# Score units moved between the halves of key and value products in a perceiver cross-attention kernel

## The chip, the cores and the metric

The kernel runs on one core of one Trainium2 chip. The metric is device time in microseconds (us) of one launch; three runs of the kernel before gave 1930.27, 1930.81 and 1931.47 us. All stage times below are of one profiled execution of the same program.

## The reference, cut to what matters

```python
x = x + xattn(layernorm(x), ctx, ctx)       # x: 256 x 512, ctx: 25088 x 512, 16 heads of 32
x = x + attn(layernorm(x))                  # linear causal attention, 256 rows
x = x + ffn(layernorm(x))                   # ternary weights, hidden 2048

def xattn(query, key, value):
    q = (query @ Wq.T).reshape(1, 256, 16, 32) * 32 ** -0.5
    k = (key @ Wk.T).reshape(1, 25088, 16, 32)
    v = (value @ Wv.T).reshape(1, 25088, 16, 32)
    scores = sigmoid(einsum('blhd,bshd->bhls', q, k))      # no softmax, so chunks of s only add up
    return einsum('bhls,bshd->blhd', scores, v).reshape(1, 256, 512) @ Wo.T
```

Only the cross-attention is touched by the change. It takes most of the time, as the 25088 rows of context are walked in chunks.

## The kernel before, in words

The context is cut into 49 chunks of 512 rows. While chunk c is scored and weighed, the keys and values of chunk c+1 are made. TensorE does four kinds of work, and they take turns in the order in which they are written in the function for TensorE:

* **Key and value products.** Keys and values of a chunk come from seven half-size block products each (a Strassen-like scheme), called K1 to K7 and V1 to V7 here. A key product (k_product, matmul at L725) is 12 matmuls of 256 columns into the one PSUM tile kp, six for its upper row block (r = 0) and six for its lower (r = 1). A value product (v_product, L746) is the same into vp. The operands are split in a rounded part and a rest, hence three terms.
* **Score units** (scores, L761): four matmuls over 96 rows into one of two PSUM tiles sc0 and sc1, which take turns. A chunk has 16 units, numbered n = 0 to 15; pair(p) issues units 2p and 2p+1. Unit n waits until the sigmoid of unit n-2 has read its tile.
* **Weighing** (weigh, L781): eight matmul instructions per unit, which multiply the sigmoids of a unit (tile probs, a ring of nine) with the values and add to acc. The units are weighed in long stretches, as a change between this kind and the others costs something.

Two chunks make one pass of the loop, 22 passes in all (chunks 1 to 44); an "odd" chunk (par 1) comes first, then an "even" one (par 0). Chunks 45 and 46 follow with the same order but without the scan described below. Chunk 0 and chunk 47 use an order of their own, called alone here, and chunk 48 only scores and weighs; the change keeps all three as they were.

What the other engines do for it, each in its own fixed order, which the change does not touch:

* **ScalarE**, per chunk: sigmoids of units 0 and 1 (L376); k_part, a copy of K1 out of kp (L380), then v_part, a copy of V1 out of vp (L384); sigmoids 2 and 3; k_first and v_first, copies after K2 and V2 (L390, L394), then the issue of the load of a later chunk of context (L482); then sigmoids 4 to 15. In the even chunk of a pass two loads of a piece of weights are issued after sigmoid 6 and two after sigmoid 14 (L469).
* **VectorE**: k_first_rest after K2 (L570). After each product i from 3 to 7 first k_summed(i), which adds kp to an earlier part (L576) and from i = 5 on also rounds the sum (L589) and takes the rest (L591), then v_summed(i), which adds vp (L597). In the even chunk v_summed(3) is followed by the combinations 1 and 2 of the chunk after the next (a cast L526 and a subtraction L513 each), v_summed(4) by combination 3 with two sums ahead of it (L500, L502, L526, L513), and v_summed(5) and v_summed(7) by two scans each of the loaded pieces (L603). Combinations 4 to 7 (with the sums L505 and L508) come at the start of the next chunk, ahead of k_first_rest.
* **SyncE** moves the rounded keys by DMA into the stacked tile that the scores read.

TensorE's products wait for the tile they write to be read: K2 waits for k_part, V2 for v_part, K3 for k_first_rest, V3 for v_first, and K_i and V_i with i over 3 for k_summed(i-1) and v_summed(i-1). In the code these are

```python
elif i == 2:
    pe.wait_ge(kt_saved, m)                      # K2: k_part on ScalarE
elif i == 3:
    pe.wait_ge(k11_lo, m + 1)                    # K3: k_first_rest on VectorE
elif i > 3:
    pe.wait_ge(k_sum, (m - 1) * 5 + (i - 3))     # K4..K7: the sum of the product before
```

Of the kernel before, what the change touches and what calls it, by code (L numbers as in the profile page):

```python
# [105 lines left out]
def cross_attention(nc, x, ctxT, wqT, wkT, wvT, woT, wqk, wv, bv, wo, w_all, biases, keep):  # L106
# [5 lines left out]
    with ExitStack() as stack:  # L112
        def sb(name, shape, dt=F32):
            return stack.enter_context(nc.sbuf_tensor(name, shape, dt))

        def sem(name):
            return stack.enter_context(nc.semaphore(name))
# [8 lines left out]
        xc = sb("x_combos", [P, 7, 2, 2, HS], F32R)  # L126
        gap("before_more_weights", 16)
        more_w = sb("more_weights", [P, 7, 2, 2, HE], F32R)
        wk, wv_c = [first_w[:, i] for i in range(7)], [more_w[:, i] for i in range(7)]
# [53 lines left out]
        x_step, x_hi, x_ready = sem("x_step"), sem("x_hi"), sem("x_ready")  # L183
        k_made, kt_saved, k11_hi, k11_lo = sem("k_made"), sem("kt_saved"), sem("k11_hi"), sem("k11_lo")
# [5 lines left out]
        v_made, vt_saved, v11_saved, v_sum = sem("v_made"), sem("vt_saved"), sem("v11_saved"), sem("v_sum")  # L190
# [46 lines left out]
        N = TC * G  # L237
# [6 lines left out]
        def place(par, n):  # L244

            return PLACE[unit_of(par, n) % RING_U]
# [446 lines left out]
        def _(pe):  # L693
            pe.wait_ge(zeros_ready, 1)
            keep_clock(nc, keep, kp[:], 11)
            for b in range(G * L // 512):
                nc.tensor.matmul(acc[:, 2 * b:2 * b + 2, :], zeros[:, 0:P], zeros[:], start=True, stop=True,
                                 skip_group_check=True)
# [8 lines left out]
            TERMS = ((0, 0), (1, 0), (0, 1))  # L707
            FRESH = (1, 3, 6)

            def k_product(m, i, first=False):  # L710
                if i == 1 and first:
                    pe.wait_ge(k_lo, 3)
                elif i == 1:
                    pe.wait_ge(k_sum, (m - 1) * 5)
                elif i == 2:
                    pe.wait_ge(kt_saved, m)
                elif i == 3:
                    pe.wait_ge(k11_lo, m + 1)
                elif i > 3:
                    pe.wait_ge(k_sum, (m - 1) * 5 + (i - 3))  # L720
                n = 0
                for r in range(2):
                    for a, b in TERMS:
                        for k in range(2):
                            last = nc.tensor.matmul(k2[:, r, :], wk[i - 1][:, k, a, r * P:(r + 1) * P],  # L725
                                                    xc[:, i - 1, k, b, :], start=i in FRESH and n == 0, stop=n == 11,
                                                    skip_group_check=True)
                            n += 1
                last.then_inc(k_made, 1)

            def v_product(m, i, first=False):
                if i == 1 and first:
                    pe.wait_ge(v0_saved, 4)
                elif i == 1:
                    pe.wait_ge(v_sum, (m - 1) * 5)
                elif i == 2:
                    pe.wait_ge(vt_saved, m)
                elif i == 3:
                    pe.wait_ge(v11_saved, m)
                elif i > 3:  # L740
                    pe.wait_ge(v_sum, (m - 1) * 5 + (i - 3))
                n = 0
                for r in range(2):
                    for a, b in TERMS:
                        for k in range(2):
                            last = nc.tensor.matmul(v2[:, r, :], xc[:, i - 1, k, b, r * P:(r + 1) * P],  # L746
                                                    wv_c[i - 1][:, k, a, :], start=i in FRESH and n == 0, stop=n == 11,
                                                    skip_group_check=True)
                            n += 1
                last.then_inc(v_made, 1)  # L750

            def scores(c, n, order, free):
                t, g = order[n]
                if free:
                    pe.wait_ge(probs_ready, c * (TC * G) + (n - 1))
                if t % 2 == 0 and g % 2 == 0:
                    q = {(0, 0): 0, (0, 2): 1, (2, 2): 2, (2, 0): 3}[t, g]
                    pe.wait_ge(lo_moved[q], c * MOVED + MOVED)
                    pe.wait_ge(hi_twice[q], c * 16 + 16)
                for j in range(HG):  # L760
                    last = nc.tensor.matmul(sc[g % 2][:, j * L:(j + 1) * L],  # L761
                                            kst[0:3 * D, t // 2, g // 2, j, g % 2, t % 2 * P:(t % 2 + 1) * P],
                                            qst[0:3 * D, j, g, :], start=True, stop=True)
                last.then_inc(scores_ready, 1)

            def weigh(c, par, units, order, first=False):
                for n in units:
                    t, g = order[n]
                    if n not in (units[0], N // 2):
                        pass  # L770
                    elif first:
                        pe.wait_ge(v0_saved, 2 if t < 2 else 4)
                    elif t < 2:
                        pe.wait_ge(v11_saved, c)
                        pe.wait_ge(v_sum, (c - 1) * 5 + 3)
                    else:
                        pe.wait_ge(v_sum, (c - 1) * 5 + 5)
                    pe.wait_ge(probs_ready, c * N + (n + 1))
                    for j in range(HG):
                        h = g * HG + j  # L780
                        last = nc.tensor.matmul(acc[D * j:D * (j + 1), g, :], v[:, par, t, h * D:(h + 1) * D],  # L781
                                                probs[:, place(par, n), j * L:(j + 1) * L], start=False, stop=False,
                                                skip_group_check=True)
                    last.then_inc(probs_used, 1)
# [55 lines left out]
            for g in range(G):  # L840
                for k in range(KE):
                    last = nc.tensor.matmul(sc[0][:, g * L:(g + 1) * L], wq_raw[:, k, g * P:(g + 1) * P],
                                            xnT[:, k, :], start=k == 0, stop=k == KE - 1)
# [8 lines left out]
            def one(c, par, first, k_next, split_next, looped):  # L852
                m = c + 1

                order = BY_HALF if k_next else BY_TILE

                def unit(n):
                    scores(c, n, order, not (first and n < 2))

                def pair(p):  # L860
                    unit(2 * p)
                    unit(2 * p + 1)

                def keys(i):
                    pe.wait_ge(x_ready, c * 7 + i)
                    k_product(m, i, first)

                if not k_next:
                    pair(0)
                    for p in range(2 * TC):  # L870
                        if p + 1 < 2 * TC:
                            pair(p + 1)
                        weigh(c, par, (2 * p, 2 * p + 1), order)
                    return
                alone = first or not split_next
                pair(0)
                keys(1)
                v_product(m, 1, first)
                pair(1)
                keys(2)  # L880
                v_product(m, 2)
                pair(2)
                if not alone and par == 0:
                    weigh(c - 1, 1, range(11, N), order)
                    weigh(c, 0, range(6), order)
                keys(3)
                v_product(m, 3)
                pair(3)
                keys(4)
                v_product(m, 4)  # L890
                if alone:
                    weigh(c, par, range(8), order, first)
                pair(4)
                keys(5)
                v_product(m, 5)
                if not alone and par == 1:
                    unit(10)
                    weigh(c, 1, range(11), order)
                    unit(11)
                else:  # L900
                    pair(5)
                keys(6)
                v_product(m, 6)
                pair(6)
                keys(7)
                pair(7)
                v_product(m, 7)
                if alone:
                    weigh(c, par, range(8, N), order, first)
                elif par == 0:  # L910
                    weigh(c, 0, range(6, N), order)

            chunks(pe, one)
            pe.wait_ge(wo_loaded, 16)

# [16 lines left out]
            for a, to in enumerate((kp, vp)):  # L932
                for g in range(G):
                    if a == 1 and g == G - 1:
                        transpose_norm(0)
                    pe.wait_ge(o_saved, g + 1)
                    last = nc.tensor.matmul(to[:], oT[:, g, a * P:(a + 1) * P], wo_sb[:, g, :],
                                            start=g == 0, stop=g == G - 1)
# [597 lines left out]
```

## Time and profile before

| | |
|---|---|
| runs | 1930.27, 1930.81, 1931.47 us |
| profiled execution | 1930.52 us, its span 1928.8 us, mean granted clock 0.999 |
| one pass (two chunks) | 68.2 to 68.4 us, 22 passes |
| PE busy / PEld busy | 99% / 89% of the span |
| DVE busy / ACT busy | 63% / 53% of the span |

PE is TensorE's matmuls, PEld its weight loads (one ahead of each matmul), DVE is VectorE, ACT is ScalarE. The ends of matmuls are modelled, so the starts of the weight loads are the better clock for TensorE: the time from the first load of one stretch to the first load of the next is what the stretch costs. In the stretches of products and scores these loads follow one another every 0.113 to 0.118 us.

### The profile page before, as it was taken

Reading aid. Unit: us, or ns where it says so; the run is one execution under the profiler, and the core shown is the slowest. Engines: PE = TensorE matmul, PEld = TensorE weight load, DVE = VectorE, ACT = ScalarE, POOL = GpSimd, SP = SyncE. Lnnn points to the kernel's source line nnn. Section 1 sums busy time; section 2 is a strip of 40 time slices with the busy share of each in tenths; the row PEclk is TensorE's granted clock in tenths of the full one; section 3 lists DMA queues with packets and bytes.
Section 4 is the critical chain, followed back from the end, with each engine's and each line's share of the span. In section 5 each row is a group of like instructions: output and inputs, shape, how many; then the busy total and the mean of one; then the engine's idle time right before and its main releaser. Section 6 shows DMA issues by size and latency. Waiting matters only on the chain. (4 is left out here: it accounts for less than half of the span.)

```text
span 1928.8 us, 50817 instructions
## 1 busy us (share of the span) xinstructions
PE 1913.4 (99%) x19362; PEld 1716.6 (89%) x19362; DVE 1212.3 (63%) x2113; ACT 1014.3 (53%) x1132; POOL 4.3 (0%) x16
## 2 busy tenths in 40 slices
PE   8999999999999999999999999999999999999999
PEld 7989999998899999989899999988999999857998
DVE  7566776767667676766767667676676766336322
ACT  5545555555545555454455555555455554544764
POOL 0000000000000000000000000000000000000000
PEclk9999999999999999999999999999999999999999
DMA  7556555665655656565565656656556564554774
GB/s 212 148 157 169 137 153 156 158 158 145 170 142 150 166 140 165 139 164 147 156 166 138 155 154 158 156 151 166 145 146 165 145 163 104 110 211 168 278 278 161
DMA packets 128395, 310.92 MB, mean 161 GB/s; under 512 B 33888, under 2 KB 33888, under 8 KB 109664
## 3 DMA queue, kind: packets, MB, share of 16 engines
q1 hardware_dynamic: 95952, 214.10, 43.8%
q10 hardware_dynamic: 32400, 96.22, 15.1%
q8 instruction: 30, 0.49, 0.1%
q14 instruction: 13, 0.11, 0.0%
HBM read 153.95 MB, written 0.52 MB: 80 GB/s over the span
## 5 line engine op out<-in xcount | busy, mean ns | idle before, releaser
L376 ACT ACTIVATE probs<-sc 128x1024 f32<-128x1024 f32 x784 | 769.4, 1025 | 719.6 <-PE sc L761 578.3
L725 PE MATMUL kp<-x_combos,weights_r 128*128 128x256 f32 x4032 | 519.7, 278 | 0.0
L746 PE MATMUL vp<-more_weights,x_combos 128*128 128x256 f32 x4032 | 518.5, 277 | 0.0
L725 PEld LDWEIGHTS kp<-x_combos,weights_r 128*128 128x128 f32 x4032 | 486.9, 188 | 9.5 <-issue 9.5
L746 PEld LDWEIGHTS vp<-more_weights,x_combos 128*128 128x128 f32 x4032 | 488.2, 188 | 0.0
L761 PE MATMUL sc<-rows_r,k_stack_r 96*128 96x256 f32 x3136 | 438.3, 281 | 0.8 <-ACT probs L376 0.8
L761 PEld LDWEIGHTS sc<-rows_r,k_stack_r 96*128 96x128 f32 x3136 | 394.2, 188 | 24.6 <-issue 21.8
L576 DVE TENSOR_TENSOR parts<-parts,kp 128x512 f32<-128x512 f32 x240 | 164.6, 686 | 321.3 <-PE kp L725 321.3
L781 PE MATMUL acc<-probs,v 128*32 128x256 f32 x6272 | 355.2, 380 | 0.0
L781 PEld LDWEIGHTS acc<-probs,v 128*32 128x32 f32 x6272 | 195.5, 110 | 131.7 <-ACT probs L376 0.4
L513 DVE TENSOR_TENSOR x_combos<-ctx_raw,x_combos 128x512 fp32r<-128x512 f32 x240 | 166.2, 692 | 8.2
L603 DVE TENSOR_TENSOR bits<-bits,weights 128x512 int32<-128x512 int32 x176 | 121.3, 689 | 45.2 <-DMA weights<-w_all_dram 41.4
L597 DVE TENSOR_TENSOR v<-parts,vp 128x512 f32<-128x512 f32 x144 | 98.7, 686 | 55.7 <-PE vp L746 55.7
L526 DVE CAST x_combos<-ctx_raw 128x512 fp32r<-128x512 f32 x240 | 101.3, 422 | 4.5 <-DMA ctx_raw<-ctxT_dram 0.8
L591 DVE TENSOR_TENSOR k_rows_lo<-parts,k_rows_hi 128x512 fp32r<-128x512 f32 x144 | 99.7, 692 | 5.0
L1306 ACT ACTIVATE w_hi<-w_raw 128x2048 fp32r<-128x2048 f32 x42 | 80.0, 1907 | 0.0
L589 DVE CAST k_rows_hi<-parts 128x512 fp32r<-128x512 f32 x144 | 61.6, 428 | 23.4 <-DMA k_stack_r<-k_rows_lo 12.3
L597 DVE TENSOR_TENSOR v<-v,vp 128x512 f32<-128x512 f32 x96 | 65.7, 684 | 10.1 <-PE vp L746 8.4
L513 DVE TENSOR_TENSOR x_combos<-x_sum,x_combos 128x512 fp32r<-128x512 f32 x96 | 66.5, 693 | 3.3
L570 DVE TENSOR_TENSOR k_rows_lo<-kp,k_rows_hi 128x512 fp32r<-128x512 f32 x48 | 33.2, 692 | 52.9 <-ACT k_rows_hi L390 52.9
L1422 PE MATMUL ps<-weights_r,w_hi 128*128 128x256 f32 x512 | 60.5, 279 | 0.0
L1422 PEld LDWEIGHTS ps<-weights_r,w_hi 128*128 128x128 f32 x512 | 60.4, 188 | 0.0
(159 smaller groups left out, 858.6 us busy)
## 6 DMA issues: line engine op xcount, KB each, us to landing
k_stack_r<-k_rows_hi SPq DMA_DIRECT2D x784, 64.0 KB, 2.4
k_stack_r<-k_rows_lo SPq DMA_DIRECT2D x784, 64.0 KB, 2.5
k_stack_r<-k_stack_r SPq DMA_DIRECT2D x196, 256.0 KB, 3.0
ctx_raw<-ctxT_dram ACTq DMA_DIRECT2D x47, 1024.0 KB, 6.4
weights<-w_all_dram ACTq DMA_DIRECT2D x176, 256.0 KB, 3.3
w_raw<-w_all_dram SPq DMA_DIRECT2D x44, 1024.0 KB, 4.8
weights<-wqk_dram SPq DMA_DIRECT2D x2, 1024.0 KB, 9.9
probs<-wkT_dram SPq DMA_DIRECT2D x2, 512.0 KB, 5.3
```

The lines of the kernel that those rows point to most:

```text
L376: nc.scalar.activation(probs[:, place(par, n), :], sc[g % 2][:], ACT.Sigmoid).then_inc(probs_ready, 1)
L513: nc.vector.tensor_tensor(xc[:, i - 1, :, 1, :], x_source(raw, i), f32(xc[:, i - 1, :, 0, :]), ALU.subtract).then_inc(x_ready, 1)
L526: nc.vector.tensor_copy(xc[:, i - 1, :, 0, :], x_source(raw, i)).then_inc(x_hi, 1)
L576: nc.vector.tensor_tensor(to, kc[:, K_PART[add], :, :], k2, ALU.add).then_inc(k_sum, 1)
L591: nc.vector.tensor_tensor(kr_lo[:, at, :, :], to, f32(kr_hi[:, at, :, :]), ALU.subtract).then_inc(k_lo, 1)
L597: nc.vector.tensor_tensor(v_at(par, q), vt[:] if add == "t" else v_at(par, add), v2, ALU.add).then_inc(v_sum, 1)
L603: nc.vector.tensor_tensor(bits[:], bits[:], piece[:, t % 2, :], ALU.bitwise_or).then_inc(piece_used, 1)
L725: last = nc.tensor.matmul(k2[:, r, :], wk[i - 1][:, k, a, r * P:(r + 1) * P], xc[:, i - 1, k, b, :], start=i in FRESH and n == 0, stop=n = ...
L746: last = nc.tensor.matmul(v2[:, r, :], xc[:, i - 1, k, b, r * P:(r + 1) * P], wv_c[i - 1][:, k, a, :], start=i in FRESH and n == 0, stop=n ...
L761: last = nc.tensor.matmul(sc[g % 2][:, j * L:(j + 1) * L], kst[0:3 * D, t // 2, g // 2, j, g % 2, t % 2 * P:(t % 2 + 1) * P], qst[0:3 * D, ...
L781: last = nc.tensor.matmul(acc[D * j:D * (j + 1), g, :], v[:, par, t, h * D:(h + 1) * D], probs[:, place(par, n), j * L:(j + 1) * L], start ...
L1422: last = nc.tensor.matmul(ps[q][:, 0, :], wt[:, k, :], x[:, k, :], start=m == 0, stop=m == passes * KH - 1)
```

## The change

TensorE's order in the odd and in the even chunk is written out anew; the alone order and the last chunk are kept. The waits themselves, every other engine's program, all tiles and the number of matmuls are kept. A product can now be issued in two calls, row block 0 (six matmuls, with the wait ahead) and row block 1 (six matmuls, with the increment behind). Let a and b be the two halves, p0 to p7 the pairs, u10 and u11 single units, W a stretch of weighing with its number of units:

```text
odd before : p0 K1 V1 p1 K2 V2 p2 K3 V3 p3 K4 V4 p4 K5 V5 u10 W11 u11 K6 V6 p6 K7 p7 V7
odd after  : K1a p0 K1b V1 p1 K2 V2 p2 K3 V3 p3 K4 V4 p4 K5 V5 u10 W11 K6a u11 K6b V6 p6 K7 V7a p7 V7b
even before: p0 K1 V1 p1 K2 V2 p2 W11 K3 V3 p3 K4 V4 p4 K5 V5 p5 K6 V6 p6 K7 p7 V7 W10
even after : K1 p0 V1 K2a p1 K2b V2 p2 W11 K3a p3 K3b V3 K4a p4 K4b V4 K5 p5 V5 K6 V6a p6 V6b K7 V7 p7 W10
```

The core of the diff:

```diff
-            def k_product(m, i, first=False):
-                if i == 1 and first:
+            def k_product(m, i, first=False, rows=(0, 1)):
+                if rows[0] == 1:
+                    pass
+                elif i == 1 and first:
...
-                n = 0
-                for r in range(2):
+                for r in rows:
+                    n = 0
                     for a, b in TERMS:
                         for k in range(2):
                             last = nc.tensor.matmul(k2[:, r, :], wk[i - 1][:, k, a, r * P:(r + 1) * P],
-                                                    xc[:, i - 1, k, b, :], start=i in FRESH and n == 0, stop=n == 11,
-                                                    skip_group_check=True)
+                                                    xc[:, i - 1, k, b, :], start=i in FRESH and r == 0 and n == 0,
+                                                    stop=r == 1 and n == 5, skip_group_check=True)
                             n += 1
-                last.then_inc(k_made, 1)
+                if rows[-1] == 1:
+                    last.then_inc(k_made, 1)
...
+                def keys_around(i, scored, n):
+                    keys(i, (0,))
+                    scored(n)
+                    keys(i, (1,))
+                def values_around(i, scored, n):
+                    values(i, (0,))
+                    scored(n)
+                    values(i, (1,))
...
+                def odd():
+                    keys_around(1, pair, 0)
+                    values(1)
+                    pair(1)
...
+                    unit(10)
+                    weigh(c, 1, range(11), order)
+                    keys_around(6, unit, 11)
+                    values(6)
+                    pair(6)
+                    keys(7)
+                    values_around(7, pair, 7)
+
+                def even():
+                    keys(1)
+                    pair(0)
+                    values(1)
+                    keys_around(2, pair, 1)
+                    values(2)
+                    pair(2)
                     weigh(c - 1, 1, range(11, N), order)
                     weigh(c, 0, range(6), order)
+                    keys_around(3, pair, 3)
+                    values(3)
+                    keys_around(4, pair, 4)
+                    values(4)
+                    keys(5)
+                    pair(5)
+                    values(5)
+                    keys(6)
+                    values_around(6, pair, 6)
+                    keys(7)
+                    values(7)
+                    pair(7)
+                    weigh(c, 0, range(6, N), order)
```

## Rows read from the trace of the kernel before

**Rows 1.** The page: busy time, share of the span and instructions of each engine.

```profile
PE 1913.4 (99%) x19362; PEld 1716.6 (89%) x19362; DVE 1212.3 (63%) x2113; ACT 1014.3 (53%) x1132; POOL 4.3 (0%) x16
```

**Rows 2.** One pass: its length, busy PE, PEld, DVE, ACT, POOL, then granted clock, DMA.

```profile
894.85:963.22 68.37, 68.37 (x724) 61.76 (x720) 46.47 (x79) 35.68 (x40) 0.00 (x0) 1.00 0.59 153
```

**Rows 3.** Timeline of PEld, odd chunk after W11: start, us, what, xcount.

```profile
918.79 0.53 PEld L761 LDWEIGHTS sc<-rows_r,k_stack_r 96*128 96x128 f32 x4 [0.41 <-issue]
919.25 1.49 PEld L725 LDWEIGHTS kp<-x_combos,weights_r 128*128 128x128 f32 x12
...
922.08 1.00 PEld L761 LDWEIGHTS sc<-rows_r,k_stack_r 96*128 96x128 f32 x8
923.00 1.44 PEld L725 LDWEIGHTS kp<-x_combos,weights_r 128*128 128x128 f32 x12
924.37 1.02 PEld L761 LDWEIGHTS sc<-rows_r,k_stack_r 96*128 96x128 f32 x8
925.32 1.49 PEld L746 LDWEIGHTS vp<-more_weights,x_combos 128*128 128x128 f32 x12
```

**Rows 4.** Timeline, start of the even chunk: ACT, then PEld.

```profile
927.62 1.94 ACT L376 ACTIVATE probs<-sc 128x1024 f32<-128x1024 f32 x2 [0.52 <-PE sc L761]
929.44 0.60 ACT L380 ACTIVATE parts<-kp 128x512 f32<-128x512 f32 x1
...
933.09 0.60 ACT L390 ACTIVATE k_rows_hi<-kp 128x512 fp32r<-128x512 f32 x1
...
926.74 1.01 PEld L761 LDWEIGHTS sc<-rows_r,k_stack_r 96*128 96x128 f32 x8
927.68 1.44 PEld L725 LDWEIGHTS kp<-x_combos,weights_r 128*128 128x128 f32 x12
929.04 1.44 PEld L746 LDWEIGHTS vp<-more_weights,x_combos 128*128 128x128 f32 x12
...
931.33 1.44 PEld L725 LDWEIGHTS kp<-x_combos,weights_r 128*128 128x128 f32 x12
```

**Rows 5.** Timeline: two waits whose release the trace shows, on PE and on DVE.

```profile
35.04 0.69 DVE L563 TENSOR_TENSOR k_rows_lo<-kp,k_rows_hi 128x512 fp32r<-128x512 f32 x1 [2.98 <-ACT k_rows_hi L420]
...
35.84 0.54 PEld L808 LDWEIGHTS kp<-x_combos,weights_r 128*128 128x128 f32 x4 [0.68 <-issue]
...
933.94 0.69 DVE L570 TENSOR_TENSOR k_rows_lo<-kp,k_rows_hi 128x512 fp32r<-128x512 f32 x1 [0.49 <-ACT k_rows_hi L390]
```

**Rows 6.** Timeline of PEld, even chunk from K3 to W10.

```profile
940.07 1.48 PEld L725 LDWEIGHTS kp<-x_combos,weights_r 128*128 128x128 f32 x12 [0.41 <-issue]
...
946.55 1.00 PEld L761 LDWEIGHTS sc<-rows_r,k_stack_r 96*128 96x128 f32 x8
...
956.20 1.02 PEld L761 LDWEIGHTS sc<-rows_r,k_stack_r 96*128 96x128 f32 x8
957.15 1.49 PEld L746 LDWEIGHTS vp<-more_weights,x_combos 128*128 128x128 f32 x12
958.77 0.16 PEld L781 LDWEIGHTS acc<-probs,v 128*32 128x32 f32 x8
```

**Rows 7.** Timeline of DVE, even chunk: the sums of V4, V5 and V6.

```profile
946.86 0.69 DVE L597 TENSOR_TENSOR v<-parts,vp 128x512 f32<-128x512 f32 x1 [0.24 <-PE vp L746]
...
951.76 0.68 DVE L597 TENSOR_TENSOR v<-parts,vp 128x512 f32<-128x512 f32 x1
...
955.64 0.68 DVE L597 TENSOR_TENSOR v<-v,vp 128x512 f32<-128x512 f32 x1
```

**Rows 8.** Timeline of DVE: second scan behind W10's start; the pass before, odd chunk.

```profile
962.34 0.69 DVE L603 TENSOR_TENSOR bits<-bits,weights 128x512 int32<-128x512 int32 x1 [0.60 <-DMA weights<-w_all_dram]
...
894.10 0.69 DVE L603 TENSOR_TENSOR bits<-bits,weights 128x512 int32<-128x512 int32 x1 [0.70 <-DMA weights<-w_all_dram]
...
899.98 0.69 DVE L513 TENSOR_TENSOR x_combos<-ctx_raw,x_combos 128x512 fp32r<-128x512 f32 x1
902.04 0.69 DVE L570 TENSOR_TENSOR k_rows_lo<-kp,k_rows_hi 128x512 fp32r<-128x512 f32 x1 [1.36 <-ACT k_rows_hi L390]
```

More of the change, by code:

```diff
@@ L725, in k_product, with v_product @@
                             last = nc.tensor.matmul(k2[:, r, :], wk[i - 1][:, k, a, r * P:(r + 1) * P],
-                                                    xc[:, i - 1, k, b, :], start=i in FRESH and n == 0, stop=n == 11,
-                                                    skip_group_check=True)
+                                                    xc[:, i - 1, k, b, :], start=i in FRESH and r == 0 and n == 0,
+                                                    stop=r == 1 and n == 5, skip_group_check=True)
                             n += 1
-                last.then_inc(k_made, 1)
-            def v_product(m, i, first=False):
-                if i == 1 and first:
+                if rows[-1] == 1:
+                    last.then_inc(k_made, 1)
+            def v_product(m, i, first=False, rows=(0, 1)):
+                if rows[0] == 1:
+                    pass
+                elif i == 1 and first:
                     pe.wait_ge(v0_saved, 4)
@@ L741, in v_product @@
                     pe.wait_ge(v_sum, (m - 1) * 5 + (i - 3))
-                n = 0
-                for r in range(2):
+                for r in rows:
+                    n = 0
                     for a, b in TERMS:
@@ L746, in v_product @@
                             last = nc.tensor.matmul(v2[:, r, :], xc[:, i - 1, k, b, r * P:(r + 1) * P],
-                                                    wv_c[i - 1][:, k, a, :], start=i in FRESH and n == 0, stop=n == 11,
-                                                    skip_group_check=True)
+                                                    wv_c[i - 1][:, k, a, :], start=i in FRESH and r == 0 and n == 0,
+                                                    stop=r == 1 and n == 5, skip_group_check=True)
                             n += 1
-                last.then_inc(v_made, 1)
+                if rows[-1] == 1:
+                    last.then_inc(v_made, 1)
             def scores(c, n, order, free):
@@ L862, in pair, with keys, values, weighing @@
                     unit(2 * p + 1)
[L864 to L868, printed above, removed]
+                def keys(i, rows=(0, 1)):
+                    if rows[0] == 0:
+                        pe.wait_ge(x_ready, c * 7 + i)
+                    k_product(m, i, first, rows)
+                def values(i, rows=(0, 1)):
+                    v_product(m, i, first, rows)
+                def keys_around(i, scored, n):
[6 more added lines that the diff above has]
+                    values(i, (1,))
+                def weighing():
                     pair(0)
@@ L873, in one, with alone @@
                         weigh(c, par, (2 * p, 2 * p + 1), order)
[L874 to L883, printed above, removed]
+                def alone():
+                    pair(0)
+                    keys(1)
+                    values(1)
+                    pair(1)
+                    keys(2)
+                    values(2)
+                    pair(2)
+                    keys(3)
+                    values(3)
+                    pair(3)
+                    keys(4)
+                    values(4)
+                    weigh(c, par, range(8), order, first)
+                    pair(4)
+                    keys(5)
[7 more added lines that the diff above has]
+                    values(7)
+                    weigh(c, par, range(8, N), order, first)
@@ new lines, in odd @@
+                def odd():
+                    keys_around(1, pair, 0)
+                    values(1)
+                    pair(1)
+                    keys(2)
+                    values(2)
+                    pair(2)
+                    keys(3)
+                    values(3)
+                    pair(3)
+                    keys(4)
+                    values(4)
+                    pair(4)
+                    keys(5)
+                    values(5)
+                    unit(10)
+                    weigh(c, 1, range(11), order)
+                    keys_around(6, unit, 11)
+                    values(6)
+                    pair(6)
+                    keys(7)
+                    values_around(7, pair, 7)
@@ L884, in one @@
+                def even():
+                    keys(1)
+                    pair(0)
+                    values(1)
+                    keys_around(2, pair, 1)
+                    values(2)
+                    pair(2)
                     weigh(c - 1, 1, range(11, N), order)
                     weigh(c, 0, range(6), order)
[L886 to L899, printed above, removed]
-                else:
[L901 to L911, printed above, removed]
+                    keys_around(3, pair, 3)
@@ new lines, in even @@
+                    values(3)
+                    keys_around(4, pair, 4)
+                    values(4)
+                    keys(5)
+                    pair(5)
+                    values(5)
+                    keys(6)
+                    values_around(6, pair, 6)
+                    keys(7)
+                    values(7)
+                    pair(7)
+                    weigh(c, 0, range(6, N), order)
+                if not k_next:
+                    weighing()
+                elif first or not split_next:
+                    alone()
+                elif par == 1:
+                    odd()
+                else:
+                    even()
```

## The prediction

> **What bounds the kernel now.** I read the page's busy times first, then one pass of the loop by stretch, then the timelines of the weight loads, of ScalarE and of VectorE within that pass. The page shows TensorE at 99% and the others at 63% and 53%, [rows 1]. One pass shows the same: PE busy 68.37 of 68.37 us, at a granted clock of 1.00, the upper level of 2.4 GHz [rows 2]. So the time is TensorE's own issue, pass after pass, and the question is how much of a pass is not plain issue. The starts of the weight loads tell it. A product costs 1.36 to 1.37 us where TensorE runs freely (927.68 to 929.04 in rows 4, 923.00 to 924.37 in rows 3), but the two just behind a stretch of weighing cost 2.83 (919.25 to 922.08), so 1.41 or 1.42 each [rows 3]: 0.05 more. A pair of scores costs 0.92 (922.08 to 923.00), but 0.95 at p7 (924.37 to 925.32), which waits a little for its sigmoids, and V7 behind it again 1.42, up to p0 at 926.74 [rows 3, 4]. Each way out of weighing costs 0.41 idle [rows 3, 6], and the new order keeps as many of them. That is all there is to win. ScalarE and VectorE are no bound by their sums, but each is a queue in fixed order, and TensorE's products wait on points in it. The margin of those waits is the real question, as none of them is late now.
>
> **What the change may win.** In the odd chunk: K1a behind weighing at the slower pace (about 0.02 lost at the head); K6a, u11, K6b, V6, p6, K7, V7a, p7, V7b without the late pair: before 926.74 - 918.79 = 7.95 [rows 3, 4], after 0.71 + 0.46 + 0.71 + 1.41 + 0.92 + 1.37 + 0.68 + 0.92 + 0.68 = 7.86, so 0.09 won. In the even chunk: from K3 to W10 before 958.77 - 940.07 = 18.70 [rows 6]; without any wait five products of each kind (13.65 at 1.365), five pairs (4.6), the 0.2 that the turn to weighing costs and some 0.07 of slower pace would give 18.52, so 0.18 won. Together 0.25 a pass. A half product is priced at half of a whole, 0.68, and at the slow pace 0.71; no row shows a split product, so the bounds for its extra cost are nothing and one more 0.05 per product (the pace of rows 3); I take nothing, as the number of switches between products and scores hardly changes.
>
> **First cost: K2 of the even chunk.** K2 must wait for k_part, which ScalarE runs only behind the sigmoids of units 0 and 1. Before, p0, K1, V1 and p1 lay between the start of p0 and K2: K2 at 931.33, k_part done at 929.44 + 0.60 = 930.04 [rows 4]. That is 3.30 after the start of p0 at 926.74, against 4.59 for K2. In the new order K1 is ahead of p0, and only p0 and V1 lie between: 0.94 + 1.36 = 2.30 after the start of p0, K2a is at its wait. The 3.30 can't shrink with K1 earlier, since 0.88 passes until the first sigmoid can start (927.62), 1.82 for the two, and 0.60 for the copy [rows 4]. On top comes the release of the wait. The nearest row is a wait of TensorE for VectorE: that one ended at 35.04 + 0.69 = 35.73, and the load came at 35.84, 0.11 later; the bounds are 0 and the 0.25 between ScalarE's end at 933.69 and VectorE's start at 933.94 [rows 4, 5]. I take 0.11, as it is the same waiting engine. So TensorE stands still for 3.41 - 2.30 = 1.11, and K2a then runs at the slow pace (0.03): 1.14 a pass, bounds 1.0 and 1.3. Queued behind K2a on TensorE are p1, K2b, V2, p2 and W11, all moved by the full amount, and nothing on another engine can give it back, because W11 and all after it are issued in order.
>
> **Second cost: V6 and V7 of the even chunk.** VectorE is busy nearly without a break from V4's sum on. V4's stretch ended at 946.55 and its sum began 0.31 later (946.86); V6's sum ended at 955.64 + 0.68 = 956.32 [rows 6, 7]. In between are combination 3, K5's and K6's sums with their splits, V5's sum and two scans, 9.46 us. With the release V7 may start 0.31 + 9.46 + 0.11 = 9.88 after V4's stretch ends. Before, TensorE took 957.15 - 946.55 = 10.60 for what lies between [rows 6], a margin of 0.72. After, p4 lies ahead of V4's end and p7 behind V7: K5, p5, V5, K6, V6a, p6, V6b, K7 take 1.37 + 0.92 + 1.36 + 1.37 + 0.68 + 0.92 + 0.68 + 1.37 = 8.67. So 1.21 of waiting, spread over the same queue: K5 and K6 wait for the sums of K4 and K5, V6a for V5's sum (done 951.76 + 0.68 - 946.86 = 5.58 after V4's began, so at 6.00 where TensorE comes at 5.02), V7 for V6's. They don't add up; the last one sets the time. From the start of K3a: V4 ends at 7.33 (K3a at slow pace 0.71, p3, K3b, V3, K4a, p4, K4b, V4), V7 starts at 7.33 + 9.88 = 17.21, takes 1.42, p7 and the turn to weighing 1.13: W10 at 19.76 against 18.70 before, 1.06 more a pass, bounds 0.9 and 1.3. This figure already holds the 0.18 that could have been won there.
>
> The Trainium skill says (Perfetto Trace Analysis, Summary: the profiler window per engine type) that the profiler's window of an engine's instruction leaves out the time in which its semaphore spreads. The 0.11 above agrees with it; by the ends of the rows alone the first stall would be 1.00. The same page (Optimizing Tensor Performance, Matmuls) advises that matmul groups take turns over PSUM banks so that the reading of one overlaps the next. Keys and values do take turns here, and by that rule alone, a read of 0.69 behind a neighbour's 1.37, the second cost would be nothing; the rows show VectorE's queue, not the tile, as what is late.
>
> **Sum.** A pass: +0.02 - 0.09 + 1.14 + 1.06 = +2.13; 22 passes give 46.9. Chunks 45 and 46 have no scans: the first cost stays 1.14, V6a still waits 0.98 of which some 0.1 is won elsewhere, so about 2.0. In all 48.9. The profiled execution took 1930.5 (span 1928.8), 0.3 below the median: forecast 1930.5 + 48.9 = 1979.4, and 1979.7 beside the median. I say 1979.5.
>
> **Rivals.** (A) Only the first cost is real: VectorE's queue catches up. For it: the queue has 0.72 of margin now. Against: p4, p5 (by its place) and p7, which made that margin, are taken from exactly this stretch. A pass would be 1.14 - 0.07 - 0.18 = +0.89, 23 times 20.5: 1951. (B) The late p7 knocks on. The loads of the scanned pieces are issued behind sigmoid 14. The second scan began 962.34 - 956.20 = 6.14 after p7 did, so 0.88 ahead of the next p0 at 963.22 [rows 2, 6, 8]; p7 then starts 1.13 ahead of W10 instead of 2.57, so the scan is 1.44 later. Combinations 4 to 7 end 6.57 after the second scan begins (894.10 to 899.98 + 0.69), so 7.13 after the pass starts; k_first_rest needs 0.69 and 0.11 more: K3 may start at 7.93, and TensorE comes at 8.25 (three pairs, four products, 0.03 of slow pace). Now k_first_rest is done at 902.73, 7.88 after the pass's start at 894.85 [rows 2, 8]: about the same margin of 0.3, behind ScalarE. If the loads land 1 us later than in this pass, K3 waits 0.7 each time: 16 more, 1996. (C) Faster: the even spacing of the pairs brings its 0.25 a pass and no wait binds: 23 x 0.25 = 6 less, 1925. It needs k_part to be done within 2.30 of p0's start and VectorE's queue within 8.67 of V4's end; for it speaks only that the late p7 and the slow pace do cost something now. It decides from a release 1.1 earlier on ScalarE, which no row allows. (D) The product halves switch dearer than priced, 0.05 for each of the seven halved products of a pass with everything else as forecast: 8 more, 1987.5.
>
> **How the numbers follow.** Forecast 0.70, A 0.12, B 0.08, C 0.03, D 0.05, and 0.02 that costs and gains cancel. The forecast's own range is 1968 to 1988, from the bounds on the releases (0 to 0.25 twice a pass) and on VectorE's queue. The range that holds 8 in 10 takes in A: 1950 to 1988. About 0.2% is what a measurement of this kernel can tell from no change. Faster by over 0.2%: C, 0.03; within: 0.02; slower: 0.95.
>
> **What would show it.** In the profile after: a row of L725 in the even chunk with some 1 us idle ahead of it, put down to ScalarE's L380, once a pass, 23 in all; idle ahead of L746 and L725 put down to VectorE's L597 and L576, about 1.2 a pass together; passes of 70.4 us in place of 68.3; V3 behind K3b at the fast 1.36; p7 of both chunks at 0.92 without a wait. The page's PE busy share would fall by about two points. If K2a follows V1 at 0.11, the first step is wrong and the whole forecast falls; if V6a and V7 follow at once, A is right; if K3 of the odd chunk shows a wait for L570, B is.

## The result, and the profile after

The changed kernel takes 1978.07 us (median of four runs, 1977.57 to 1978.87) against 1931.06 before: ratio 1.0248, 95% interval 1.0236 to 1.0260. The forecast was 1979.5, within 1950 to 1988. A few runs of most kernels are 4 to 6 us lower than the rest (1925.33 beside a median of 1931.20 for the kernel before) and stay in the medians, and one of the kernel before, 3016.06 us at a granted clock of 0.592, is left out of the ratios.

First the page of the profile after: span, busy times, clock. PE does the same matmuls and loses a point of its share, but its busy time grows by 25.8 us: the rows of matmuls stretch over part of the waiting, so the starts of the weight loads are again the better clock. The granted clock is 1.000 in the mean, its upper level.

```profile
span 1976.4 us, 50816 instructions
PE 1939.2 (98%) x19361; PEld 1727.4 (87%) x19362; DVE 1209.8 (61%) x2113; ACT 1012.6 (51%) x1132; POOL 4.3 (0%) x16
PEclk9999999999999999999999999999999999999999
```

One pass of the loop by stretch (its length, then busy PE, PEld, DVE, ACT, POOL, the clock, DMA). It answers to [rows 2]: 70.31 us where a typical pass took 68.24, and PE is no longer busy throughout. (The 68.37 of [rows 2] is one of three passes of the kernel before that are 0.13 longer than its others.)

```profile
919.60:989.91 70.31, 69.33 (x725) 62.10 (x721) 46.19 (x78) 35.58 (x40) 0.00 (x0) 1.00 0.59 149
```

Twenty-two passes at 2.07 more are 45.5 us, and the last odd and even chunk without scans bring the rest of 47.0: W10 of chunk 46 began at 1688.4 in place of 1641.1. From the start of the last W10 to the end the two kernels take nearly the same, 288.0 and 287.7.

**The first place: K2a of the even chunk.** The timeline of the weight loads (start, duration as merged, what, count), then that of ScalarE over the same stretch. It answers to [rows 4].

```profile
951.25 1.48 PEld L728 LDWEIGHTS kp<-x_combos,weights_r 128*128 128x128 f32 x12
952.66 1.00 PEld L769 LDWEIGHTS sc<-rows_r,k_stack_r 96*128 96x128 f32 x8
953.59 1.48 PEld L753 LDWEIGHTS vp<-more_weights,x_combos 128*128 128x128 f32 x12
956.07 0.76 PEld L728 LDWEIGHTS kp<-x_combos,weights_r 128*128 128x128 f32 x6 [1.00 <-DVE x_combos L513]
...
960.85 4.47 PEld L789 LDWEIGHTS acc<-probs,v 128*32 128x32 f32 x88
...
953.53 1.94 ACT L376 ACTIVATE probs<-sc 128x1024 f32<-128x1024 f32 x2 [1.19 <-PE sc L769]
955.35 0.60 ACT L380 ACTIVATE parts<-kp 128x512 f32<-128x512 f32 x1
```

V1 takes from 953.59 to 956.07, 2.48 in place of 1.36: a hole of 1.12 ahead of K2a. The copy of K1 (L380) ends at 955.95 by its row, and the load comes 0.12 later; unrounded, and over 22 passes, it is 0.11 each time. The row of the load itself names VectorE's L513, which is a trap: two waits stand ahead of K2a, one for combination 2 of the context (L513) and one for the copy of K1. Combination 2 was ready at 941.41; the instruction of L513 that ended shortly before K2a belongs to a later combination. The list of waits of TensorE (engine, line, waited for: us in total, times, longest) has both:

```profile
PE kp L728 <- ACT parts L380: 18.9, 23, 0.8
```

```profile
PEld kp L728 <- DVE x_combos L513: 22.9, 23, 1.0
PEld vp L753 <- DVE v L597: 7.1, 23, 0.3
PEld kp L728 <- DVE parts L576: 5.6, 22, 0.3
```

Both counts are 23, once in each even chunk; that the copy is the true releaser was settled by moving it (below).

**The second place: K3 to W10 of the even chunk.** It answers to [rows 6, 7]: weight loads, then VectorE.

```profile
965.74 0.78 PEld L728 LDWEIGHTS kp<-x_combos,weights_r 128*128 128x128 f32 x6 [0.41 <-issue]
...
971.73 1.44 PEld L753 LDWEIGHTS vp<-more_weights,x_combos 128*128 128x128 f32 x12
973.19 1.48 PEld L728 LDWEIGHTS kp<-x_combos,weights_r 128*128 128x128 f32 x12
...
975.52 1.48 PEld L753 LDWEIGHTS vp<-more_weights,x_combos 128*128 128x128 f32 x12
977.26 1.48 PEld L728 LDWEIGHTS kp<-x_combos,weights_r 128*128 128x128 f32 x12 [0.26 <-DVE parts L576]
979.05 0.77 PEld L753 LDWEIGHTS vp<-more_weights,x_combos 128*128 128x128 f32 x6 [0.31 <-DVE v L597]
...
982.92 1.47 PEld L753 LDWEIGHTS vp<-more_weights,x_combos 128*128 128x128 f32 x12
...
985.45 1.66 PEld L789 LDWEIGHTS acc<-probs,v 128*32 128x32 f32 x34
```

```profile
973.40 0.69 DVE L597 TENSOR_TENSOR v<-parts,vp 128x512 f32<-128x512 f32 x1 [0.27 <-PE vp L753]
...
976.53 0.68 DVE L576 TENSOR_TENSOR parts<-parts,kp 128x512 f32<-128x512 f32 x1
...
978.31 0.68 DVE L597 TENSOR_TENSOR v<-parts,vp 128x512 f32<-128x512 f32 x1
...
982.18 0.68 DVE L597 TENSOR_TENSOR v<-v,vp 128x512 f32<-128x512 f32 x1
```

The stretch takes 985.45 - 965.74 = 19.71, against 18.70 before. K6 comes at 977.26, 0.05 after K5's sum (977.21); V6a at 979.05, 0.06 after V5's (978.99); V7 at 982.92, 0.06 after V6's (982.86). Ahead of K5, K6, V6a and V7 the weight loads are late by 0.10, 0.33, 0.38 and 0.12, 0.93 in all. From V3's sum to V6's, VectorE waits for TensorE only once, the 0.27 ahead of V4's sum. The stretch is 1.01 longer, though the waits come to 0.93: the rest is a slower pace of some products, to which I come below.

### The profile page after: what moved, and what is told of

Its sections match the earlier page's. It is cut to its first block and busy times, and to the rows that moved or that the text cites. A ratio compares the mean times of both kernels' runs of the same rounds, so it can differ in the third digit from the quotient of the medians.

```text
span 1976.4 us, 50816 instructions
## 1 busy us (share of the span) xinstructions
PE 1939.2 (98%) x19361; PEld 1727.4 (87%) x19362; DVE 1209.8 (61%) x2113; ACT 1012.6 (51%) x1132; POOL 4.3 (0%) x16
## 5 line engine op out<-in xcount | busy, mean ns | idle before, releaser
L728 PE MATMUL kp<-x_combos,weights_r 128*128 128x256 f32 x4032 | 554.0, 282 | 20.1 <-ACT parts L380 18.9
L728 PEld LDWEIGHTS kp<-x_combos,weights_r 128*128 128x128 f32 x4032 | 498.8, 188 | 57.7 <-issue 28.6
L753 PE MATMUL vp<-more_weights,x_combos 128*128 128x256 f32 x4032 | 530.1, 279 | 2.4
L769 PE MATMUL sc<-rows_r,k_stack_r 96*128 96x256 f32 x3136 | 432.1, 279 | 0.8 <-ACT probs L376 0.8
L513 DVE TENSOR_TENSOR x_combos<-ctx_raw,x_combos 128x512 fp32r<-128x512 f32 x240 | 166.2, 693 | 8.2
L513 DVE TENSOR_TENSOR x_combos<-x_sum,x_combos 128x512 fp32r<-128x512 f32 x96 | 66.4, 692 | 3.3
```

The source lines that it names most:

```text
L513: nc.vector.tensor_tensor(xc[:, i - 1, :, 1, :], x_source(raw, i), f32(xc[:, i - 1, :, 0, :]), ALU.subtract).then_inc(x_ready, 1)
L769: last = nc.tensor.matmul(sc[g % 2][:, j * L:(j + 1) * L], kst[0:3 * D, t // 2, g // 2, j, g % 2, t % 2 * P:(t % 2 + 1) * P], qst[0:3 * D, ...
```

## The experiments

Each kernel's time is a median; the kernel before, run beside each on the same chip, had medians of 1930.3 to 1931.4. All are the changed kernel with the edit shown unless it is said otherwise, and all keep the computation whole. The edits are shortened: calls that stand on lines of their own in the code share one here, and "..." marks a cut.

**K2 whole again, with p1 ahead of it.**

```diff
 def even():
-    keys(1); pair(0); values(1); keys_around(2, pair, 1); values(2); pair(2)
+    keys_around(1, pair, 0); values(1); pair(1); keys(2); values(2); pair(2)
```

> The changed kernel with the head of the even chunk written as K1a p0 K1b V1 p1 K2 V2 p2 in place of K1 p0 V1 K2a p1 K2b V2 p2: K2 gets p1 back ahead of it, all else as changed. Theory 1 (K2 waits for ScalarE's copy of K1, 1.12 us in each of 23 even chunks): K2 comes 3.88 us after p0 starts, the copy is released at 3.41, so the wait goes; p0 is now 2.3 behind p7 and may wait some 0.1 for sigmoid 15. 1978.1 - 23 x 1.05 = 1954. Theory 2 (VectorE's queue alone costs the time, and the wait at K2a only shifts it): the stretch from K3 to W10 would grow by what is won, 1978.

Measured 1951.2, a pass 69.15 in place of 70.31. The hole is gone, the stretch from K3 to W10 is unchanged at 19.7, so theory 2 is out and theory 1 holds. The time came out 3 lower than expected: p0 didn't wait (0.93), and V1 is at the fast pace again (1.36).

**The copy of K1 first, TensorE's order untouched.**

```diff
+early = par == 0 and split_next and not first
+if n == 0 and early:
+    k_part(m)
 sigmoid(c, par, n, at, first)
 if k_next and n == 1:
-    k_part(m)
+    if not early:
+        k_part(m)
```

> The changed kernel with TensorE's order untouched, and ScalarE's copy of K1 (k_part) put ahead of sigmoid 0 in the even chunks. Theory 1 (what is late at K2a is the copy's place in ScalarE's queue, behind two sigmoids): the copy is done 0.9 us after p0 starts, K2a follows V1 at once, 1978.1 - 23 x 1.14 = 1952. Theory 2 (what costs is K2 cut in two around a pair of scores, by itself): the gap at K2a stays and the time is 1978.

Measured 1954.0, a pass 69.26. ScalarE's and TensorE's rows at the place that had the hole:

```profile
940.32 0.60 ACT L380 ACTIVATE parts<-kp 128x512 f32<-128x512 f32 x1 [0.64 <-PE kp L732]
940.88 1.94 ACT L376 ACTIVATE probs<-sc 128x1024 f32<-128x1024 f32 x2
...
940.93 1.48 PEld L757 LDWEIGHTS vp<-more_weights,x_combos 128*128 128x128 f32 x12
942.35 0.78 PEld L732 LDWEIGHTS kp<-x_combos,weights_r 128*128 128x128 f32 x6
```

V1 to K2a is 1.42: no hole, though K2 is still cut around p1, VectorE's combinations are where they were, and only ScalarE's order changed. So the copy's place behind two sigmoids was the cause, neither the cut nor L513. The 0.05 to 0.06 over 1.36 is the slow pace; of the hole of 1.12 it leaves 1.07 of standing still.

**The second part of the even chunk as before.** K3 V3 p3 K4 V4 p4 K5 V5 p5 K6 V6 p6 K7 p7 V7 in place of the new order from K3 on.

> The changed kernel with the even chunk's second part, K3 to p7, in the order of the kernel before (K3 V3 p3 K4 V4 p4 K5 V5 p5 K6 V6 p6 K7 p7 V7); heads and odd chunk as changed. Theory 1 (two independent costs, 1.12 at K2a and 1.00 between K3 and W10): that stretch goes from 19.70 back to 18.70 us, 1978.1 - 23 x 1.0 = 1955, and K2a still waits 1.12. Theory 2 (one cost that the other follows from): near 1931 or no change, 1978.

Measured 1955.05: the stretch from K3 to W10 takes 18.66, and V1 to K2a still 2.48. The two costs are independent and add: 1978.1 - 1951.2 = 26.9 for the head and 23.0 for this part. Their sum, 49.9, is 2.9 more than the 47.0 of the change, as both runs keep the odd chunk's new order, which wins something: 31.65 us from its start to that of the even chunk in place of 31.76, 0.11 a pass or 2.5 in all.

**p4 behind V4.**

```diff
-    keys_around(4, pair, 4); values(4)
+    keys(4); values(4); pair(4)
```

> The changed kernel with one pair moved: K4 V4 p4 in the even chunk in place of K4a p4 K4b V4. Theory 1 (VectorE needs 9.88 us from the end of V4's stretch to V7, whatever stands between): V4 ends at 6.41 after K3a in place of 7.43, V7 may start at 16.29 in place of 17.2, TensorE's own work is 9.59 long there, so 0.3 of waiting is left of 1.2: W10 at 18.83 in place of 19.70, 1978.1 - 23 x 0.87 = 1958. Theory 2 (the waits belong to the split products or to the pairs' distance from their sigmoids): one pair's place changes little, 1974 to 1978.

Measured 1970.1: 8 us less, where theory 1 expected 20 and theory 2 at most 4. The weight loads behind V3, V4 and K7, then VectorE's timeline, say why.

```profile
965.24 1.48 PEld L728 LDWEIGHTS kp<-x_combos,weights_r 128*128 128x128 f32 x12
...
968.06 1.01 PEld L769 LDWEIGHTS sc<-rows_r,k_stack_r 96*128 96x128 f32 x8
...
978.39 1.48 PEld L753 LDWEIGHTS vp<-more_weights,x_combos 128*128 128x128 f32 x12
...
965.55 0.69 DVE L597 TENSOR_TENSOR v<-parts,vp 128x512 f32<-128x512 f32 x1 [0.68 <-PE vp L753]
...
968.28 0.68 DVE L576 TENSOR_TENSOR parts<-parts,kp 128x512 f32<-128x512 f32 x1
968.88 0.68 DVE L597 TENSOR_TENSOR v<-parts,vp 128x512 f32<-128x512 f32 x1
...
977.66 0.68 DVE L597 TENSOR_TENSOR v<-v,vp 128x512 f32<-128x512 f32 x1
```

V4 ended at 968.06, but its sum could not start until 968.88: VectorE was on V3's sum, combinations 1 and 2 and K4's sum without a break from 965.55 on. So V7 is bound twice. Here it comes 13.15 after V3's end (965.24 to 978.39) and 10.33 after V4's. In the changed kernel VectorE has the break of 0.27 ahead of V4's sum, so there V4's end binds, 9.83 ahead of V7 (973.09 to 982.92), and the bound from V3's end lies 0.36 earlier (969.41 + 13.15 = 982.56). With p4 moved back the bound from V3 takes over after 0.36; what is left of the cost belongs to p3 ahead of V3. The prediction had priced the bound that holds in the changed kernel, not the one close behind it.

**p3 behind V3, p4 between the halves of K4.**

```diff
-    keys_around(3, pair, 3); values(3)
+    keys(3); values(3); pair(3)
```

> The changed kernel with one pair moved: K3 V3 p3 in the even chunk in place of K3a p3 K3b V3; p4 stays between the halves of K4. What the run with p4 moved showed (1970 where 1958 was expected): VectorE's queue is busy from V3's sum on, so V7 is bound twice, by 13.2 us from the end of V3's stretch and by 9.88 from the end of V4's. Theory 1 (two bounds): V3's end comes 0.9 earlier but V4's stays, so nothing is won, 1977 to 1978. Theory 2 (p3 ahead of V3 is what costs, p4 doesn't matter): 13 us less, 1965.

Measured 2008.0, far outside both. The edit left only half a product between p3 and p4, and the waits of the weight loads show a new kind, which I had not looked for. The list of waits, then one even chunk from K4a to V7:

```profile
PEld sc L769 <- ACT probs L376: 26.6, 51, 0.9
```

```profile
985.26 0.76 PEld L728 LDWEIGHTS kp<-x_combos,weights_r 128*128 128x128 f32 x6
986.36 0.53 PEld L769 LDWEIGHTS sc<-rows_r,k_stack_r 96*128 96x128 f32 x4 [0.34 <-ACT probs L376]
987.61 0.53 PEld L769 LDWEIGHTS sc<-rows_r,k_stack_r 96*128 96x128 f32 x4 [0.72 <-ACT probs L376]
988.08 0.78 PEld L728 LDWEIGHTS kp<-x_combos,weights_r 128*128 128x128 f32 x6
...
990.19 1.48 PEld L728 LDWEIGHTS kp<-x_combos,weights_r 128*128 128x128 f32 x12
...
1000.01 1.47 PEld L753 LDWEIGHTS vp<-more_weights,x_combos 128*128 128x128 f32 x12
```

p4 begins 0.4 late and takes 1.71 in place of 0.92, as its units wait for the sigmoids of p3: 1.2 of the 1.3 that a pass is longer (71.61 for 70.31). The time can't decide between the two theories. The trace does bear on the first: counted from K3, V4 ends 1.33 later than in the changed kernel, and V7 comes 9.82 behind it (990.19 to 1000.01), the 9.83 of the changed kernel, though VectorE now stood idle for 1.64 between V3's sum and K4's. So the bound from V4's end holds by itself.

**Both pairs behind their value products.** K3 V3 p3 K4 V4 p4, from K5 on as changed.

> The changed kernel with both pairs moved: K3 V3 p3 K4 V4 p4 in the even chunk, and from K5 on as changed. Theory 1 (two bounds, from V3 and from V4): both are back where they were, some 0.2 of waiting is left in the stretch from K3 to W10, 18.8 in place of 19.70 us, 1978.1 - 23 x 0.9 = 1957, though either pair alone gives 8 or nothing. Theory 2 (the two moves add up, 8 for p4 and nothing for p3): 1970.

Measured 1958.75, the stretch from K3 to W10 18.84 us. So p3 and p4 ahead of V3 and V4 together make 0.86 of the second cost, and p4 alone, moved back, 0.34 (8 us). Theory 1 was off by 1.8, theory 2 by 11. The 0.14 over the 18.70 of before is not the waiting that was expected: no wait of TensorE for VectorE is left in the list, and it is the slow pace.

**Combination 3 late, TensorE's order untouched.**

```diff
-combos = ... {3: (1, 2), 4: (3,)}
+combos = ... {3: (1, 2), 7: (3,)}
```

> The changed kernel with TensorE's order untouched; on VectorE combination 3 of the even chunk (four instructions, 2.5 us) is moved from behind V4's sum to behind V7's, ahead of the two scans whose loads it waits for there. Theory 1 (V6 and V7 wait for VectorE's queue, which has dead time only behind V7's sum): V5's and V6's sums come 2.5 us earlier, of 0.93 waiting some 0.1 to 0.15 stays at K5 (combinations 1 and 2), and the scans still end when their loads land: 1978.1 - 23 x 0.8 = 1960. Theory 2 (the waits belong to the split products): no change, 1978; and if the dead time is needed, the next chunk's K3 waits, up to 1990.

Measured 1960.45, a pass 69.53. The waits at K6, V6a and V7 are gone, and the one at K5 (0.10) stays as expected. VectorE at the end of the even chunk:

```profile
975.30 0.68 DVE L597 TENSOR_TENSOR v<-v,vp 128x512 f32<-128x512 f32 x1
975.90 0.68 DVE L500 TENSOR_TENSOR ctx_raw<-ctx_raw 128x512 f32<-128x512 f32 x1
...
979.13 0.69 DVE L603 TENSOR_TENSOR bits<-bits,weights 128x512 int32<-128x512 int32 x1 [0.63 <-DMA weights<-w_all_dram]
```

The four instructions now fill the time in which VectorE stood waiting for the pieces; in the changed kernel that wait was 2.73 long at the first scan. The second cost is thus VectorE's queue, not the halves. But the prediction's rival B shows itself here: in four of 22 passes the loaded pieces land so late that the second scan begins 1.04 to 1.34 into the next pass (at most 0.80 in the changed kernel), and K3 of that odd chunk waits for k_first_rest, by up to 0.34:

```profile
849.32 1.48 PEld L728 LDWEIGHTS kp<-x_combos,weights_r 128*128 128x128 f32 x12 [0.27 <-DVE k_rows_lo L570]
```

**Both cures, and combination 1 early.** First the copy first and combination 3 late together; then also combination 1 of the even chunk behind the two scans at its start.

> The changed kernel with TensorE's order untouched, ScalarE's copy of K1 ahead of sigmoid 0 and VectorE's combination 3 behind V7's sum, both in the even chunks. Theory (the order itself is worth some 0.2 us a pass, and only the two queues took it back): no wait is left but 0.1 to 0.15 at K5, a pass takes 68.2 us as before or a little less, 1926 to 1931 against 1930.3 of the kernel before. Rival (the cures cost what they free elsewhere): 1935 to 1945.

> As the kernel with both cures, and combination 1 of the even chunk is moved from behind V3's sum to behind the scans at its start, in VectorE's idle stretch during W11. Theory: the wait at K5 goes too, a pass takes some 68.0 us, 1924 to 1927. Rival: the load of the context lands too late there and K4 waits for K3's sum, 1930 or more.

Measured 1936.15 (ratio to before 1.0029, interval 1.0018 to 1.0040) and 1934.87 (1.0022, 1.0012 to 1.0031). Both theories missed, and both times lie where the rivals had put them, though mostly not for the rivals' reasons. In the typical pass every wait but K5's 0.10 is gone in the first, K5's too in the second, and still a pass takes 68.46 and 68.37 where the kernel before has 68.24. In the second the odd chunk takes 0.11 less than before, but K1 to W11 takes 8.56 for 8.44 and K3 to W10 18.81 for 18.71, all of it slow pace. So the new order by itself costs 0.13 a pass; it does not win 0.25. What the rivals feared comes in single passes and adds under 1 us to the profiled executions: K3 of the odd chunk is late in two of 22 passes of the first run (by up to 0.24) and one of the second, and in two of the second K4 waits 0.4 for K3's sum, behind a combination 1 that waits for its load of the context.

The profiled execution of the second run took 1930.34, less than its median. Its passes are the 68.37 above; what is short is the time from the start of the last W10 to the end, 283.8 us in place of 288.1 in the first. The cause was not looked for.

**Where the expected gain went.** In all these traces the products run at two paces, 0.1135 and 0.1178 us a matmul (1.36 and 1.41 a product), and where no wait stands the slow one begins at the same places: where a value product or half of one follows scores (V6b, V7b, V7 of the kernel before), and where a key product follows a value product with no scores between (V7b K1, V3 K4a, V4 K5, V6b K7). It ends where a key product follows scores or goes on behind them. It also begins behind W11 (K3a and K6a take 0.70). To test it away from waits, one pair was moved in the kernel before, in the odd chunk, where there is room:

```diff
-    values(3); pair(3); keys(4)
+    values_around(3, pair, 3); keys(4)
```

> The kernel before with one pair moved in the odd chunk: V3a p3 V3b K4 in place of V3 p3 K4. No wait binds there by a wide margin for K4 (2.3 us after K3 ends, its sum needs 1.1). Theory 1 (the slow pace of 0.118 us a matmul starts where a value product follows scores or a key product follows a value product with no scores between, and ends where a key product follows scores): V3b takes 0.706, K4 and V4 1.41 each, fast again from K5 on; 0.12 a pass, 1931 + 2.7 = 1934. Theory 2 (the slow pace is left over from a wait or a late semaphore): V3b 0.68, K4 1.36 as before, at most V4 slow, 1931 to 1932.

Measured 1934.26 (1.0016, interval 1.0004 to 1.0029). The weight loads from V3a to V5:

```profile
906.19 0.76 PEld L753 LDWEIGHTS vp<-more_weights,x_combos 128*128 128x128 f32 x6
906.87 1.00 PEld L769 LDWEIGHTS sc<-rows_r,k_stack_r 96*128 96x128 f32 x8
907.79 0.78 PEld L753 LDWEIGHTS vp<-more_weights,x_combos 128*128 128x128 f32 x6
908.50 1.48 PEld L728 LDWEIGHTS kp<-x_combos,weights_r 128*128 128x128 f32 x12
909.91 1.49 PEld L753 LDWEIGHTS vp<-more_weights,x_combos 128*128 128x128 f32 x12
911.33 1.00 PEld L769 LDWEIGHTS sc<-rows_r,k_stack_r 96*128 96x128 f32 x8
912.25 1.44 PEld L728 LDWEIGHTS kp<-x_combos,weights_r 128*128 128x128 f32 x12
```

V3a 0.68, V3b 0.71, K4 1.41, V4 1.42, and K5 behind p4 1.37 again, in all 22 passes: as theory 1 said, at this place. Why a matmul is 0.004 dearer there is not shown, and the pattern is not a full rule. K6 behind the single unit u11, straight after weighing, is slow in the kernel before (1.415), while K1a behind W10 is fast in the changed one (0.68). K1 and V1 of the odd chunk, behind p0, are slow in 3 of 22 passes of the kernel before and in 9 of 22 of this run, with the same order in every pass. And a wait can start the slow pace too: K3 behind a late p2 takes 1.40 to 1.41 in four passes of the run with combination 3 late. So theory 2 is out for V3b and K4, not as a second cause elsewhere.

**The kernel before with what was found.** From the changed order only K6a u11 K6b in the odd chunk, and combination 3 late, which takes away the small wait of V6; else the kernel before.

> The kernel before with two things taken over: K6a u11 K6b in place of u11 K6 in the odd chunk, and VectorE's combination 3 behind V7's sum in the even chunk. From the changed kernel's table, K6 and V6 behind W11 cost 3.22 us in place of 3.29, and without the small wait V6 of the even chunk (1.40) goes to 1.36: 0.10 to 0.12 a pass, 1931 - 2.6 = 1928. Rival (the halves and the place of the combination bring nothing of their own): 1930 to 1931.

Measured 1927.39 in eleven runs against 1931.38, ratio 0.9973, interval 0.9962 to 0.9984: small, but faster than both kernels. A pass takes 68.12 in place of 68.24: K6 and V6 with u11 take 3.22 in place of 3.29, and V6 of the even chunk 1.36 in place of 1.41. The half behind W11 ends the slow pace at once (K6b 0.69, V6 1.36).

## Why the prediction was right

**The wait at K2a.** Predicted 1.11 of standing still, measured a hole of 1.12; from K1 to W11 9.58 forecast, 9.60 measured. K2a came 3.41 after p0, as forecast, and the release after ScalarE is the 0.11 that was taken from a wait for VectorE. One moved copy takes the hole away, so the mechanism is shown. The step left out the slow pace of K1 and V1 (1.41 each in the run with the copy first). V1's is hidden in the hole; K1's is about what the stretch came out dearer.

**VectorE's queue.** From K3 to W10 19.76 forecast, 19.71 measured, with V7 17.21 after the start forecast and 982.92 - 965.74 = 17.18 measured; all four waits named appeared. VectorE's 9.46 from V4's sum to the end of V6's came out to the digit. The release after VectorE is 0.05, half of the 0.11 taken. But the step was less complete than its number: it named one bound of V7, from V4's end, and a second one, from V3's end, lay 0.36 behind it. By the prediction's own rule the run with p4 moved should have won 20; it won 8.

**The gain.** The 0.25 a pass was the wrong term. Of it, the shorter turn behind W11 is real (u11 and K6, V6: 3.22 in place of 3.29, and p6, K7 and p7 without delay), but the step read the slow V7 as the leftover of a late p7. The run with V3 halved shows the same slow pace behind scores that were not late. The new order makes more such places than it takes away, so without any wait it stands at 0.13 above the kernel before.

**The sum.** The odd chunk was forecast at -0.07 and measured at -0.11, K1 to W11 at +1.14 and +1.18, K3 to W10 at +1.06 and +0.99: 2.13 forecast, 2.07 measured. Each part is near, but that the wrong gain hardly shows is partly luck: under the two long waits part of the slow pace costs nothing, and the release on VectorE was priced too high.

**The rivals.** A (only the first cost) is out: both are there, 27 and 23. B (odd K3 late) did not come, by a small margin: the second scan began at 990.63, 0.73 into the next pass, where 0.56 was worked out, and k_first_rest ended 0.3 ahead of K3's turn. Over 22 passes the scan began no later than 0.80; where it began at 1.04 or later, in the run with combination 3 late, K3 did wait. C needed both queues to be done early, and even so would not have been faster, as the run with both cures shows. D had a trace of truth in the slow halves, at 0.025 each.

**The signs.** The share of PE fell by one point where about two were forecast, as PE's rows hide part of the waiting. The list of waits leaves out the small ones at K5 and V7 and names 0.55 a pass for VectorE (7.1 and 5.6 over 23 chunks); the starts of the loads show 0.93, and the prediction said about 1.2. The copy (L380) is named only in the row of the matmul, not in that of the weight load.

## What to carry to other kernels

When work on a full engine is put in another order, the order's own worth is read last; first list, for each wait in it, what the other engines' fixed queues do until they release it, and how much time the new order leaves between. A margin belongs to a stretch of such a queue, and the stretch begins where that queue last had a break, not at the instruction that is moved; when the break closes, an earlier stretch takes over. Where the new order is to stay, look for the other queue's dead time: here one copy moved on ScalarE and four instructions on VectorE took back 42 of 47 us.

## What the runs showed of the hardware

* Two paces of the same matmul at the full clock, 0.1135 and 0.1178 us. In the places looked at without a wait, a value product behind scores or a key product straight behind a value product starts the slow one; other places don't follow this. Not expected, and its cause is open.
* In the loop of the changed kernel the release of TensorE came 0.11 after ScalarE's end (K2a) and mostly 0.05 after VectorE's (K5, K6, V6a, V7). In the one case ahead of the loop that the prediction used it came 0.11 after VectorE's.
* While TensorE waits, the rows of its matmuls can cover part of the waiting: a pass has 0.98 without a busy PE, and weight loads that come 2.0 late.
